# Expert results written to rows of their own, read back and summed at the end, in a GNN + mixture-of-experts kernel

## The chip, the cores and the metric

The kernel runs on one core of a Trainium2 chip. The metric is the device time of one execution in microseconds (us), smaller is better. Data are float32 throughout, except for a few index and bf16 helper tiles.

## The reference

Two layers over 1024 nodes of width 512. The first is a graph layer; the second is a mixture of 64 experts, of which each token takes the best two, with a small shared expert beside them:

```
x = x + relu(segment_sum(w[e] * (layernorm(x) @ W)[dst[e]], src[e]) + bias)   # 16384 edges
t = layernorm(x)                                                              # the ffn's input
scores = sigmoid(t @ Wg.T + bg);  w, idx = top_k(scores, 2);  w = w / w.sum(-1)
nx = layernorm(t)
y[token] = sum over its 2 experts e of  w_e * ( (silu(h1_e) * h3_e) @ W2_e + b2_e )
           h1_e = (nx*gamma_e + beta_e) @ W1_e + b1_e     # 512 -> 256
           h3_e = (nx*gamma_e + beta_e) @ W3_e + b3_e
z = shared expert of width 32;  out = x + y + z
```

So there are 1024 x 2 = 2048 pairs of token and expert, 32 for an expert on average. Each expert has 1.5 MB of weights (W1, W3 and W2 of 512 KB each), 96 MB in all, and each is read once.

## The kernel before, in words

The work has three stages. Up to about 130 us the graph layer is built from one-hot products. Up to about 190 us the tokens are routed: every token's two experts and weights are found, and a record (token, weight) is scattered to the DRAM table `slots`, in which each expert has a list of CAP = 80 entries (empty ones hold 60000). From about 193 us to the end the 64 experts run, in 8 groups (`GROUPS`) of 8 (`RING`). This last stage is the one that the change touches.

For each expert u of a group, five engines work in a chain, tied by semaphores:

- SP (SyncE) loads the expert's weights into a ring of 8 buffers (`load_expert`, lines 278 to 280). The load for the expert 8 further on is issued when the second matmul of this one is done (`y_ps`).
- POOL (GpSimd) gathers the 80 rows of the expert's tokens from `nx_rows` in DRAM by an indirect DMA (`gather`, line 443) into one of 8 buffers `xg`, six experts ahead (`AHEAD`). Empty entries lie past the bound and move nothing.
- PE (TensorE) transposes these rows (line 1074), multiplies by W1 and W3 (`up`, line 1098) and by W2 (`down`, line 1105). Its order is: rows of u+1, up of u, down of u-1.
- DVE (VectorE) applies gamma and beta (line 871) and forms silu(h1)*h3 (line 887). ACT (ScalarE) computes the silu (line 598) and, in `result` (line 607), scales the expert's result by the routing weight into one of 4 buffers `ysb`. Before it may overwrite one, it waits on `y_out` for the scatter of four experts earlier.
- POOL scatters `ysb` to the DRAM table `totals` with an accumulating indirect DMA (`scatter`, line 452). `totals` holds one row for each token, prefilled with the rest of the output (`store_x`, line 303), and 80 spare rows to which the empty entries go. Since two experts may add to the same row, each scatter first waits until the one before it has landed.

POOL runs all of its part in one order. For a step u of a group: gather(u+6), then scatter(u-1). At the start of each group it waits for its gathers and copies the gather indices (line 472), waits until all scatters of the group before have landed, copies the scatter indices (line 480), and only then issues gather(6) of the new group. After the last scatter SP copies `totals` from DRAM to the output in one DMA (line 324).

Of the kernel before, what the change touches and what calls it, by code (L numbers as in the profile page):

```python
# [6 lines left out]
N, D = 1024, 512  # L7
# [3 lines left out]
P = 128  # L11
NB = N // P
# [10 lines left out]
CAP = 80  # L23
# [3 lines left out]
RING = 8  # L27
GROUPS = EXPERTS // RING
XG, AHEAD = 8, 6
YS = 4  # L30
# [3 lines left out]
def moe_gnn(nc, x, src, dst, ew, W, bias, Wg, bg, gamma, beta, W1, b1, W3, b3, W2, b2,  # L34
# [11 lines left out]
    f32, i32, u32, bf16 = mybir.dt.float32, mybir.dt.int32, mybir.dt.uint32, mybir.dt.bfloat16  # L46
    ALU = mybir.AluOpType
# [5 lines left out]
    with ctx:  # L53
# [3 lines left out]
        def sem(name):  # L57
            return ctx.enter_context(nc.semaphore(name))
# [1 line left out]

        nx_rows = nc.dram_tensor("nx_rows", (N, D), f32).ap()
        slots = nc.dram_tensor("slots", (EXPERTS * LIST, REC), f32).ap()
        totals = nc.dram_tensor("totals", (N + CAP, D), f32).ap()


        w13 = sb("w13", [P, RING, 2, DC, HID])
        w2 = sb("w2", [P, RING, HC, D])
        X = sb("X", [P, NB, D])
        A = sb("A", [P, (N + WIN) * 8])
        HW = sb("HW", [P, NB, D])  # L70
# [16 lines left out]
        spare = sb("spare", [P, 1])  # L87
# [49 lines left out]
        before = GW[:, 0, 256:384]  # L137
        stackT = [GW[0:97, 2 + i // 4, 128 * (i % 4):128 * (i % 4) + 128] for i in range(NB)]
        late = A[:, :]
# [15 lines left out]
        idx_g = late[0:CAP, o + 192:o + 192 + RING + AHEAD].bitcast(i32)  # L155
        idx_s = late[0:CAP, o + 208:o + 208 + RING].bitcast(i32)

        mv1 = small[:, 0:16].rearrange("p (s a) -> p s a", a=2)
        ve = small[:, 16:32].rearrange("p (s a) -> p s a", a=2)
        rs = small[:, 32:48].rearrange("p (s a) -> p s a", a=2)  # L160
# [71 lines left out]
        xe_ps, xe_ready, h_ps, sl_ready, hT_ready, y_ps, y_ready = (sem(s) for s in (  # L232
            "xe_ps", "xe_ready", "h_ps", "sl_ready", "hT_ready", "y_ps", "y_ready"))
        y_out = [sem(f"y_out{i}") for i in range(YS)]
        x_out = sem("x_out")
        out_done = sem("out_done")
        held = sem("held")

        def hold(engine):

            engine.sem_inc(held, 1)
# [8 lines left out]
        def _(sp):  # L250
# [21 lines left out]
            sp.wait_ge(consts, 6)  # L272
            sp.dma_start(slots.rearrange("(p n) r -> p (n r)", p=P), sentinel).then_inc(sentinel_out, 16)

            sp.dma_start(totals[N:N + CAP, :], HW[0:CAP, 0, :]).then_inc(sentinel_out, 16)

            def load_expert(e, u):
                sp.dma_start(w13[:, u, 0, :, :].rearrange("p c h -> p (c h)"), W1v[e]).then_inc(w_in[u], 16)
# [18 lines left out]
                sp.wait_ge(rec_out[i], 32 * NB // 2)  # L297
            lists = slots.rearrange("(e n) r -> e (n r)", e=EXPERTS)

            def store_x(blocks):  # L300
                for s in blocks:
                    sp.wait_ge(z_added, s + 1)
                    sp.dma_start(totals[s * P:(s + 1) * P, :], X[:, s, :]).then_inc(x_out, 16)

            with sp.Fori(0, R2) as r:
                sp.dma_start(L, lists[:, ds(r * (CAP * REC), CAP * REC)]).then_inc(list_in, 16)
                with sp.If(r < 1):
                    store_x(range(NB))
                with sp.Fori(0, GROUPS - 1) as g:
                    for u in range(RING):  # L310
                        used = sp.snap(r * EXPERTS + g * RING + (u + 1))
                        e = sp.snap(g * RING + (RING + u))
                        sp.wait_ge(y_ps, used)
                        load_expert(e, u)
                with sp.If(r + 1 < R2):
                    for u in range(RING):
                        used = sp.snap(r * EXPERTS + (EXPERTS - RING + u + 1))
                        sp.wait_ge(y_ps, used)
                        load_expert(u, u)

            last = sp.snap(R2 * (16 * EXPERTS // YS))
            for i in range(YS):
                sp.wait_ge(y_out[i], last)
            sp.dma_start(out.rearrange("(p b) d -> p (b d)", p=P),
                         totals[0:N, :].rearrange("(p b) d -> p (b d)", p=P)).then_inc(out_done, 16)
            sp.wait_ge(out_done, 16)


        @block.gpsimd
        def _(pool):  # L330
# [12 lines left out]

            g.memset(rec, 0.0).then_inc(consts, 1)
            pool.wait_ge(consts, 7)
            g.iota(rec[:, :, :, 0], pattern=[[P, NB], [0, 2]], base=0, channel_multiplier=1,
                   allow_small_or_imprecise_dtypes=True).then_inc(consts, 1)
            pool_n = [0]

# [56 lines left out]
            def scatter_records(s):  # L406

                pool.wait_ge(rec_ready, s + 1)
                if s == 0:
                    pool.wait_ge(sentinel_out, 32)  # L410
                for k in range(2):
                    g.indirect_dma_start(slots, bass.IndirectOffsetOnAxis(ap=slot[:, s, k:k + 1], axis=0),  # L412
                                         rec[:, s, k, :], None).then_inc(rec_out[s % 2], 16)
# [29 lines left out]
                g.indirect_dma_start(xg[b], None, nx_rows, bass.IndirectOffsetOnAxis(ap=idx_g[:, col:col + 1], axis=0),  # L443
                                     bounds_check=N - 1, oob_is_err=False).then_inc(xg_in[b], 16)

            def scatter(u, count, before):

                pool.wait_ge(y_ready, count)
                if u:
                    pool.wait_ge(y_out[(u - 1) % YS], (before + (u - 1) // YS + 1) * 16)  # L450
                hold(pool)
                g.indirect_dma_start(totals, bass.IndirectOffsetOnAxis(ap=idx_s[:, u:u + 1], axis=0), ysb[u % YS], None,  # L452
                                     compute_op=ALU.add).then_inc(y_out[u % YS], 16)

            with pool.Fori(0, R2) as r:
                pool.wait_ge(list_ready, r + 1)
# [7 lines left out]
                def group(gi, first, last):  # L464
                    n = RING if last else RING + AHEAD
                    base = r * EXPERTS + gi * RING
                    before = r * (EXPERTS // YS) + gi * (RING // YS)

                    for b in range(AHEAD):
                        pool.wait_ge(xg_in[b], (r * GROUPS + gi + 1) * 16)  # L470
                    hold(pool)
                    g.tensor_copy(idx_g[:, 0:n], TOK[:, ds(gi * RING, n)]).then_inc(idx_copied, 1)
                    if first:
                        pool.wait_ge(x_out, 16 * NB)
                        hold(pool)
                    else:
                        for b in range(YS):
                            pool.wait_ge(y_out[b], before * 16)
                        hold(pool)
                    g.tensor_copy(idx_s[:, :], DROW[:, ds(gi * RING, RING)]).then_inc(idx_copied, 1)  # L480
                    pool.wait_ge(idx_copied, r * (2 * GROUPS + 1) + gi * 2 + 3)
                    hold(pool)
                    for u in range(RING):
                        if not (last and u >= RING - AHEAD):
                            if not first or u + AHEAD >= XG:

                                pool.wait_ge(xe_ps, base + (u + AHEAD - XG + 1))
                                hold(pool)
                            gather(u + AHEAD, (u + AHEAD) % XG)
                        if u:  # L490
                            scatter(u - 1, base + u, before)
                    scatter(RING - 1, base + RING, before)

                group(0, True, False)
                with pool.Fori(1, GROUPS - 1) as gi:
# [7 lines left out]
        def _(act):  # L503
# [17 lines left out]

            def x_times_w(g, u):
                act.wait_ge(hw_ps, g + 1)
                act.wait_ge(sentinel_out, 32)
                a.copy(HW[:, ds(g, 1), :].rearrange("p a n -> p (a n)"), bank[6 + u][:, :]).then_inc(hw_ready, 1)

            def pair(j, last):
# [95 lines left out]
        def _(dve):  # L623
# [231 lines left out]
            R2 = dve.value_load(rounds_sb[0:1, 1:2], min_val=1, max_val=ROUNDS)  # L855
            with dve.Fori(0, R2) as r:
                dve.wait_ge(list_ps, r + 1)
                v.tensor_copy(TOK, bank[6][0:CAP, 0:64])
                v.tensor_scalar(DROW, bank[6][0:CAP, 0:64], spare[0:CAP, :], None, ALU.min)
                v.tensor_copy(CW, bank[6][0:CAP, 64:128]).then_inc(list_ready, 1)  # L860
                with dve.If(r < 1):
                    for b in range(3, 6):
# [31 lines left out]
                group(GROUPS - 1, True)  # L894
                for i in range(YS):
                    dve.wait_ge(y_out[i], (r + 1) * (16 * EXPERTS // YS))

        @block.tensor
        def _(pe):
# [244 lines left out]
```

## Time and profile before

| | us |
|---|---|
| median of 3 runs | 652.58 |
| lowest and highest run | 644.8, 663.48 |
| span of the profiled execution, first to last instruction | 654.0 |

The profiled execution has no time listed apart from its span. Its span lies 1.4 us above the median of the runs. Of the span PE is busy 567.6 us (87%), POOL 233.9 us (36%), DVE 225.0 us (34%) and ACT 174.2 us (27%). PE's matmuls are pipelined, so that its busy time is no measure of its peak; the stretches in which it has no work at all, and those in which its clock is below 1.0, are what is to be looked for.

### The profile page before, as it was taken

To read this page: it belongs to the slowest core of one execution; us is meant where nothing else is said; L and a number is where in the kernel's file an instruction comes from. 1 tells how busy PE (TensorE), PEld (TensorE's weight loads), DVE (VectorE), ACT (ScalarE), POOL (GpSimd) and SP (SyncE) were. 2 spreads that over 40 slices of the span, in tenths; PEclk is the share of its full clock that TensorE was granted. 3 is DMA by queue.
4 is the path that set the end of the run, shared out by engine and by line. 5 is a ranking of instruction groups with operands and counts; after the bars stand their busy time and mean duration, and the time that the engine had idled before them with its cause. 6 is when DMAs were issued, how large, how long until landed. Compare 5 with 4: busy or idle time off the path is not lost. (4 is left out here: it accounts for less than half of the span.)

```text
span 654.0 us, 10918 instructions
## 1 busy us (share of the span) xinstructions
PE 567.6 (87%) x3327; PEld 425.4 (65%) x3328; DVE 225.0 (34%) x816; ACT 174.2 (27%) x399; POOL 233.9 (36%) x308
## 2 busy tenths in 40 slices
PE   4999999999639999899959999886997997799940
PEld 3666665566327888678846877665886785688820
DVE  5767622676744233222312322221232222122200
ACT  9698842232201212212202112110211121022110
POOL 3744401333625322332244232415323431542331
PEclk9899999999858999969968999895998899599975
DMA  5992001000013899969867998794998799494224
GB/s 171 407 401 85 0 5 42 33 18 32 33 40 125 270 319 305 287 201 325 283 185 230 308 299 272 235 299 133 289 317 264 214 295 307 84 324 127 40 30 148
DMA packets 53402, 127.23 MB, mean 195 GB/s; under 512 B 9832, under 2 KB 10408, under 8 KB 53218
## 3 DMA queue, kind: packets, MB, share of 16 engines
q1 hardware_dynamic: 42626, 112.24, 48.6%
q0 software_dynamic: 10752, 14.72, 13.3%
q8 instruction: 10, 0.16, 0.1%
q14 instruction: 14, 0.11, 0.1%
HBM read 117.82 MB, written 17.49 MB: 207 GB/s over the span
## 5 line engine op out<-in xcount | busy, mean ns | idle before, releaser
L1098 PE MATMUL bank<-A,w 128*128 128x80 f32 x2048 | 255.4, 286 | 0.0
L1098 PEld LDWEIGHTS bank<-A,w 128*128 128x128 f32 x2048 | 253.1, 204 | 0.5 <-issue 0.5
L452 POOL DMA_INDIRECT totals<-A x64 | 91.9, 1435 | 231.8 <-issue 141.5
L1105 PE MATMUL bank<-w,A 128*80 128x512 f32 x256 | 126.9, 626 | 3.3 <-DVE A L887 3.3
L871 DVE TENSOR_SCALAR A<-bank,gT,bT 128x80 f32<-128x80 f32 x256 | 74.6, 353 | 106.8 <-PE bank L1074 106.8
L887 DVE SCALAR_TENSOR_TENSOR A<-bank,b13T,A 128x80 f32<-128x80 f32 x128 | 32.6, 296 | 210.3 <-ACT A L598 210.3
L598 ACT ACTIVATE A<-bank,b13T 128x80 f32<-128x80 f32 x128 | 34.7, 323 | 237.3 <-PE bank L1098 237.3
L1074 PEld LDWEIGHTS bank<-ident,A 80*128 80x128 f32 x256 | 39.8, 210 | 63.3 <-DMA A<-nx_rows,A 36.3
L607 ACT ACTIVATE A<-bank,A 80x512 f32<-80x512 f32 x64 | 43.7, 682 | 116.1 <-PE bank L1105 67.4
L443 POOL DMA_INDIRECT A<-nx_rows,A x64 | 62.6, 978 | 26.2 <-issue 24.4
L1105 PEld LDWEIGHTS bank<-w,A 128*80 128x80 f32 x256 | 36.2, 160 | 47.2 <-issue 39.3
L1074 PE MATMUL bank<-ident,A 80*128 80x80 f32 x256 | 39.4, 278 | 30.1 <-DMA A<-nx_rows,A 30.1
L987 PE MATMUL bank<-HW,AT 128*128 128x512 f32 x128 | 57.3, 593 | 0.0
L513 ACT ACTIVATE osl<-iota,eT 128x128 f32<-128x128 f32 x128 | 39.0, 388 | 10.9 <-PE bank L950 10.9
L987 PEld LDWEIGHTS bank<-HW,AT 128*128 128x128 f32 x128 | 23.3, 190 | 23.9 <-issue 23.9
L957 PE MATMUL bank<-GW,xhT 128*128 128x512 f32 x64 | 29.7, 609 | 0.0
L715 DVE TENSOR_TENSOR A<-A,bank 128x384 f32 x32 | 17.7, 553 | 27.1 <-PE bank L950 23.9
L384 POOL TENSOR_SCALAR M<-iota,small 128x128 f32<-128x128 f32 x16 | 13.6, 852 | 24.8 <-PE bank L950 24.1
L950 PE MATMUL bank<-M,osl 128*128 128x128 f32 x128 | 20.2, 305 | 0.0
L412 POOL DMA_INDIRECT slots<-small,GW x16 | 16.5, 1029 | 10.3 <-DVE GW L833 6.3
L957 PEld LDWEIGHTS bank<-GW,xhT 128*128 128x128 f32 x64 | 12.0, 199 | 12.0 <-issue 12.0
L950 PE MATMUL bank<-AT,osl 128*128 128x128 f32 x128 | 19.3, 296 | 0.0
(166 smaller groups left out, 381.4 us busy)
## 6 DMA issues: line engine op xcount, KB each, us to landing
w<-in_L_ffn_W_dram SPq DMA_DIRECT2D x192, 512.0 KB, 5.9
X<-in_x_dram SPq DMA_DIRECT2D x4, 512.0 KB, 6.3
totals<-X SPq DMA_DIRECT2D x8, 256.0 KB, 2.9
GW<-in_L_gnn_W_dram SPq DMA_DIRECT2D x1, 1024.0 KB, 9.4
nx_rows<-osl SPq DMA_DIRECT2D x4, 256.0 KB, 2.0
nx_rows<-xh SPq DMA_DIRECT2D x4, 256.0 KB, 2.0
A<-nx_rows,A POOLq DMA_INDIRECT x64, 5.0
totals<-A POOLq DMA_INDIRECT x64, 5.1
```

The costliest lines, as they stand in the source:

```text
L443: g.indirect_dma_start(xg[b], None, nx_rows, bass.IndirectOffsetOnAxis(ap=idx_g[:, col:col + 1], axis=0), bounds_check=N - 1, oob_is_err=F ...
L452: g.indirect_dma_start(totals, bass.IndirectOffsetOnAxis(ap=idx_s[:, u:u + 1], axis=0), ysb[u % YS], None, compute_op=ALU.add).then_inc(y_ ...
L513: ins = a.activation(osl[:, h % 2, k, :], iota[:, :], ACT.Abs, bias=eT[:, 1, ds(j * 32 + 8 * h + k, 1)])
L598: ins = a.activation(sl[u % 2][:, m, :], bank[2 + u % 2][:, m * CAP:(m + 1) * CAP], ACT.Silu, bias=b13T[:, 0, m, ds(g * RING + u, 1)])
L607: a.activation(ysb[u % YS], bank[6 + u % 2][0:CAP, :], ACT.Copy, scale=CW[:, ds(g * RING + u, 1)]).then_inc(y_ready, 1)
L871: ins = v.tensor_scalar(xe[b][:, c, :], bank[b][:, c * CAP:(c + 1) * CAP], gT[:, c, ds(e, 1)], bT[:, c, ds(e, 1)], ALU.mult, ALU.add)
L950: ins = t.matmul(bank[q % 4][:, ds(at[k], TW)], osl[:, (q // 2) % 2, (q % 2) * QUAD + k, :], Mq[q % 4][:, k, :], start=False, stop=(k == Q ...
L957: ins = t.matmul(bank[6 + u][:, :], xhT[:, u, c, :], GW[:, c, :], start=(c == 0), stop=(c == DC - 1))
L987: ins = t.matmul(bank[4 + s % 2][:, :], AT[:, s % 2, k, :], HW[:, k, :], start=(k == 0), stop=(k == NB - 1))
L1074: ins = t.transpose(bank[u % 2][:, c * CAP:(c + 1) * CAP], xg[u % XG][:, c:c + DC * (P - 1) + 1:DC], ident[0:CAP, 0:CAP])
L1098: ins = t.matmul(bank[b][:, m * CAP:(m + 1) * CAP], w13[:, u, a, c, m * P:(m + 1) * P], xe[u % 2][:, c, :], start=(c == 0), stop=(c == DC ...
L1105: ins = t.matmul(bank[6 + u % 2][0:CAP, :], hT[u % 2][:, m, :], w2[:, u, m, :], start=(m == 0), stop=(m == HC - 1))
```

## The change

Each result now goes to a row of its own. The record of a token's first choice holds the token number, that of its second choice the token number plus 1024, and `totals` has 2048 rows. The scatter writes without accumulation and without a wait for the scatter before it, and empty entries lie past a bound, so they move nothing. DVE works out the token number from the record with one more instruction. `totals` is no longer prefilled: X with the shared expert's part stays in SBUF. At the end SP reads `totals` back in 8 DMAs of 512 KB (both rows of 128 tokens each) into weight buffers, DVE adds the two rows to X (two instructions for each block), and SP stores each block with a DMA of 256 KB. The waits at the start of a group, and ACT's wait on `y_out`, stay.

```
-        totals = nc.dram_tensor("totals", (N + CAP, D), f32).ap()
+        totals = nc.dram_tensor("totals", (2 * N, D), f32).ap()
...
+        token_of = late[0:CAP, o + 216:o + 280]
+        back = [w13[:, 2 + i // 2, i % 2, :, :].rearrange("p c h -> p (c h)").rearrange("p (k d) -> p k d", k=2) for i in range(NB)]
...
-            sp.dma_start(totals[N:N + CAP, :], HW[0:CAP, 0, :]).then_inc(sentinel_out, 16)
...
-                with sp.If(r < 1):
-                    store_x(range(NB))
...
-            sp.dma_start(out.rearrange("(p b) d -> p (b d)", p=P),
-                         totals[0:N, :].rearrange("(p b) d -> p (b d)", p=P)).then_inc(out_done, 16)
-            sp.wait_ge(out_done, 16)
+            for s in range(NB):
+                sp.dma_start(back[s], totals.rearrange("(k n) d -> n k d", k=2)[s * P:(s + 1) * P, :, :]).then_inc(back_in[s], 16)
+            for s in range(NB):
+                sp.wait_ge(x_final, s + 1)
+                sp.dma_start(out[s * P:(s + 1) * P, :], X[:, s, :]).then_inc(out_done, 16)
+            sp.wait_ge(out_done, 16 * NB)
...
-            g.iota(rec[:, :, :, 0], pattern=[[P, NB], [0, 2]], base=0, channel_multiplier=1,
+            g.iota(rec[:, :, :, 0], pattern=[[P, NB], [N, 2]], base=0, channel_multiplier=1,
...
-            def scatter(u, count, before):
+            def scatter(u, count):
                 pool.wait_ge(y_ready, count)
-                if u:
-                    pool.wait_ge(y_out[(u - 1) % YS], (before + (u - 1) // YS + 1) * 16)
                 hold(pool)
                 g.indirect_dma_start(totals, bass.IndirectOffsetOnAxis(ap=idx_s[:, u:u + 1], axis=0), ysb[u % YS], None,
-                                     compute_op=ALU.add).then_inc(y_out[u % YS], 16)
+                                     bounds_check=2 * N - 1, oob_is_err=False).then_inc(y_out[u % YS], 16)
...
-                    if first:
-                        pool.wait_ge(x_out, 16 * NB)
-                        hold(pool)
-                    else:
+                    if not first:
                         for b in range(YS):
                             pool.wait_ge(y_out[b], before * 16)
                         hold(pool)
...
-                v.tensor_copy(TOK, bank[6][0:CAP, 0:64])
-                v.tensor_scalar(DROW, bank[6][0:CAP, 0:64], spare[0:CAP, :], None, ALU.min)
+                v.tensor_scalar(token_of, bank[6][0:CAP, 0:64], float(N), -float(N), ALU.is_ge, ALU.mult).then_inc(second_half, 1)
+                v.tensor_copy(DROW, bank[6][0:CAP, 0:64])
+                dve.wait_ge(second_half, r + 1)
+                v.tensor_tensor(TOK, token_of, bank[6][0:CAP, 0:64], ALU.add)
...
+            for s in range(NB):
+                dve.wait_ge(back_in[s], 16)
+                link(v.tensor_tensor(X[:, s, :], back[s][:, 0, :], X[:, s, :], ALU.add))
+                v.tensor_tensor(X[:, s, :], back[s][:, 1, :], X[:, s, :], ALU.add).then_inc(x_final, 1)
```

## Rows read from the trace of the kernel before

**Rows 1.** The page's 40 slices: PE's busy tenths, granted clock in tenths

```profile
PE   4999999999639999899959999886997997799940
...
PEclk9899999999858999969968999895998899599975
```

**Rows 2.** Waits, whole span: engine, line, releaser: us in total, times, longest

```profile
POOL totals L452 <- DMA totals<-A: 62.2, 17, 5.6
ACT A L607 <- DMA totals<-A: 48.7, 15, 8.4
...
PEld bank L1074 <- DMA A<-nx_rows,A: 36.3, 8, 8.8
```

**Rows 3.** Timeline of PE, expert stage: start us, us, engine, line, count, idle before

```profile
203.35 3.76 PE L1098 MATMUL bank<-A,w 128*128 128x80 f32 x32
...
241.72 3.74 PE L1098 MATMUL bank<-A,w 128*128 128x80 f32 x32
...
249.16 3.74 PE L1098 MATMUL bank<-A,w 128*128 128x80 f32 x32
...
327.21 1.88 PE L1105 MATMUL bank<-w,A 128*80 128x512 f32 x4
336.37 0.81 PE L1074 MATMUL bank<-ident,A 80*128 80x80 f32 x4 [7.28 <-DMA A<-nx_rows,A]
336.97 7.03 PE L1098 MATMUL bank<-A,w 128*128 128x80 f32 x32
...
347.64 3.74 PE L1098 MATMUL bank<-A,w 128*128 128x80 f32 x32
...
621.21 3.69 PE L1098 MATMUL bank<-A,w 128*128 128x80 f32 x32
```

**Rows 4.** Timelines of ACT (first row) and POOL, experts 8 to 16

```profile
302.84 0.68 ACT L607 ACTIVATE A<-bank,A 80x512 f32<-80x512 f32 x1 [1.55 <-DMA totals<-A]
...
276.56 1.45 POOL L452 DMA_INDIRECT totals<-A  x1 [0.30 <-issue]
...
326.32 1.42 POOL L452 DMA_INDIRECT totals<-A  x1 [6.11 <-issue]
...
331.65 0.18 POOL L480 COPY A<-A 80x8 int32 x1 [3.71 <-DMA totals<-A]
332.93 1.01 POOL L443 DMA_INDIRECT A<-nx_rows,A  x1 [1.09 <-issue]
```

**Rows 5.** View of the tensor totals, 250 to 600 us

```profile
DMA to landing us min/median/max: 3.8/5.6/8.3
```

**Rows 6.** DMA views: whole span; 14 to 50 us; one stretch (engines, clock, DMA share, GB/s)

```profile
q1 hardware_dynamic: 42626, 112.24, 48.6%
q0 software_dynamic: 10752, 14.72, 13.3%
...
DMA packets 5071, 14.55 MB, mean 404 GB/s; under 512 B 436, under 2 KB 436, under 8 KB 4938
...
360.00:370.00 10.00, 10.00 (x78) 8.82 (x77) 3.26 (x12) 1.77 (x5) 2.41 (x2) 1.00 0.99 315
```

**Rows 7.** Timelines of ACT, POOL and SP, last two groups

```profile
593.04 0.68 ACT L607 ACTIVATE A<-bank,A 80x512 f32<-80x512 f32 x1 [1.31 <-PE bank L1105]
...
594.52 1.44 POOL L452 DMA_INDIRECT totals<-A  x1 [6.23 <-ACT A L607]
...
628.48 0.68 ACT L607 ACTIVATE A<-bank,A 80x512 f32<-80x512 f32 x1 [1.03 <-PE bank L1105]
...
641.22 1.40 POOL L452 DMA_INDIRECT totals<-A  x1 [3.28 <-DMA totals<-A]
645.22 0.63 SPq L324 DMA_DIRECT2D out_dram<-totals  x1
```

**Rows 8.** DVE: groups by line; timeline at 195.7 us

```profile
L837 DVE TENSOR_TENSOR X<-X,bank 128x512 f32<-128x512 f32 x8 | 5.2, 683 | 3.3 <-PE bank L1031 3.3
...
195.72 0.27 DVE L859 TENSOR_SCALAR A<-bank,spare 80x64 int32<-80x64 f32 x1
```

More of the change, by code:

```diff
@@ L234, in moe_gnn @@
         y_out = [sem(f"y_out{i}") for i in range(YS)]
-        x_out = sem("x_out")
+        back_in = [sem(f"back_in{i}") for i in range(NB)]
+        x_final = sem("x_final")
         out_done = sem("out_done")
+        second_half = sem("second_half")
         held = sem("held")
@@ L298, in _ @@
             lists = slots.rearrange("(e n) r -> e (n r)", e=EXPERTS)
[L300 to L303, printed above, removed]
             with sp.Fori(0, R2) as r:
                 sp.dma_start(L, lists[:, ds(r * (CAP * REC), CAP * REC)]).then_inc(list_in, 16)
-                with sp.If(r < 1):
-                    store_x(range(NB))
                 with sp.Fori(0, GROUPS - 1) as g:
@@ L409, in scatter_records @@
                 if s == 0:
-                    pool.wait_ge(sentinel_out, 32)
+                    pool.wait_ge(sentinel_out, 16)
                 for k in range(2):
@@ L490, in group @@
                         if u:
-                            scatter(u - 1, base + u, before)
-                    scatter(RING - 1, base + RING, before)
+                            scatter(u - 1, base + u)
+                    scatter(RING - 1, base + RING)
                 group(0, True, False)
@@ L523, in x_times_w @@
                 act.wait_ge(hw_ps, g + 1)
-                act.wait_ge(sentinel_out, 32)
+                act.wait_ge(sentinel_out, 16)
                 a.copy(HW[:, ds(g, 1), :].rearrange("p a n -> p (a n)"), bank[6 + u][:, :]).then_inc(hw_ready, 1)
```

## The prediction, made before the changed kernel ran

> **What bounds the kernel now.** I read the 40 slices of the page first [rows 1]. PE is at 9 tenths for most of the span, so the kernel looks bound by TensorE. But in the second half there are dips, and the clock row falls to 5 or 6 tenths near each. The list of waits says who makes them [rows 2]: PE's weight loads wait 36.3 us in 8 places for the DMA that gathers token rows. The same list shows POOL waiting 62.2 us for its own last scatter, and ACT waiting 48.7 us for a scatter to free its result buffer.
>
> The timeline of PE turns this into a floor [rows 3]. From the first product of expert 0 (203.35) to that of expert 8 (249.16) nothing stops it: 45.81 us for a group of 8, or 5.73 us an expert, at full clock. From expert 0 to expert 7 it is 38.37 us. Without a stop the last expert would start 7 x 45.81 + 38.37 = 359.0 us after the first, at 562.4. It starts at 621.21. So 58.8 us are lost.
>
> One stop shows how. PE starts the second product of expert 19 at 327.21, behind the first of expert 20; then it is idle 7.28 us until the rows of expert 22 are there (336.37). When it goes on, its clock is at the lower of its two levels (1.2 GHz instead of 2.4): the products of expert 21 take 7.03 us instead of 3.74, and from there to the next expert it is 347.64 - 336.97 = 10.67 us instead of 5.73, so 4.9 us more. I found the same pattern, a late row gather in the sixth step of a group, six times, with the lower clock after five of them; and one more stop, of 5.0 us in all, where ACT waited for a buffer. With the longer products behind each, the six cost 7.5, 12.6, 1.5, 12.2, 8.4 and 12.2 us (rows 3 show the second). All seven give 59.4 us, which agrees with the 58.8.
>
> Why is the gather late? POOL's timeline answers [rows 4]. The eight scatters of experts 8 to 15 start between 276.56 and 326.32, 7.1 us apart, while PE needs 5.73 for an expert. A scatter waits for the landing of the one before; with its issue of 1.45 us and a landing of 5.6 us in the median [rows 5] that is the 7.1. ACT had expert 15's result at 302.84 + 0.68 = 303.5, and its scatter starts at 326.32, 22.8 us late. Only after it has landed does POOL copy the new group's indices (331.65) and issue the gather of expert 22 (332.93), for which PE is already waiting. The chain of accumulating scatters sets the pace, by way of POOL's fixed order.
>
> **The change, part by part.** *The wait between scatters goes.* POOL's work for an expert is then one gather and one scatter, 1.01 + 1.45 us and 0.3 us before each: 3.1 us, against 5.73 for PE. POOL stops being late within a group. What stays is the start of a group: the last scatter, its landing, two copies, two gathers. In rows 4 the gather follows the last scatter after 332.93 - 326.32 = 6.6 us and the next scatter some 9 us after it; this is under two experts' time, and ACT has four buffers. How early is the gather of a group's seventh expert then? Expert 7's result is out when expert 8 starts, near 250, its scatter starts about 1 us later, the gather of expert 14 near 258, and it has landed by 263. PE wants those rows ahead of expert 13's product, five experts after 249.16, at about 276. There are 13 us of slack. ACT's wait for a buffer asks for a scatter four experts back, 4 x 5.73 = 22.9 us, against issue plus landing of about 7 to 10 us. So neither wait should ever end last, and the whole 58.8 us go, the low-clock stretches included, since in this trace (experts 0 to 12) the clock stays at 1.0 while PE has no stop. Bounds: nothing at all to 58.8; I take 58.8 because both slacks are larger than any landing shown (8.3 at most, rows 5).
>
> *What is late next?* PE itself, if DMA can follow. The weight queue moved 112.24 MB in 48.6% of 654 us [rows 6], 353 GB/s; 1.57 MB of weights are 4.5 us an expert. The indirect queue took 13.3%, 87 us, or 1.3 us for each of 64 experts. Together 5.8 us, which fills PE's 5.73, and the stretch at 360 us indeed shows a DMA share of 0.99. Afterwards the indirect queue moves fewer bytes: gathers 2048 rows of 2 KB (4.2 MB), scatters 2048 rows instead of 64 x 80 = 5120 (4.2 MB instead of 10.5): 8.4 instead of 14.7 MB. By bytes alone that is 0.8 us an expert, 5.3 in all; an add costs more than a write if anything. So DMA drops below PE's pace, with 8% to spare, and landings should get shorter. If scatters were no cheaper than now, DMA would lose 0.07 us an expert, 5 us in all: that is a bound for the range.
>
> *The prefill goes* (8 stores of 256 KB before the first expert, and 160 KB at the start). Nobody on the path waits for them: the list of waits has no line in which POOL or PE waits for the prefill. I cost it at nothing, 0 to 1 us of gain. The weight loads behind them on SP's queue wait for PE anyway.
>
> *DVE's extra instruction* stands before the first gathers. Its like takes 0.27 us [rows 8]; with the semaphore I take +0.3 us. PE is covered by the shared expert's matmuls until the first rows come, so it is 0 to 0.6.
>
> *The end.* Now: ACT's last result is out at 628.48 + 0.68 = 629.16 [rows 7], but the scatters lag behind by 12 us, and the last starts at 641.22; SP issues the output copy at 645.22, and the end is at 654.0. That is 24.8 us after the result. Afterwards: a scatter starts 0.8 us after its result when POOL is free (593.04 + 0.68 to 594.52), and 4.0 us after its start SP goes on (641.22 to 645.22): 4.8 us. Then 4.2 MB are read and 2.1 MB written. The largest stretch of plain loads of this size ran at 404 GB/s [rows 6]: 6.3 MB are 15.6 us. The output copy's 8.8 us for 2.1 MB (5.2 us at that rate) leave 3.5 us of fixed cost, so 19 us. DVE gives nearly the same: first block landed after 3.5 + 1.3, then 8 blocks x 2 adds x 0.68 us [rows 8] plus 0.1 for the link, 11.7 us, then one store's 2 to 3 us: 19. The end takes 4.8 + 19 = 23.8 us, 1.0 less than now. The drain of the chain pays for the reading back. Bounds: 3 us better, if an unaccumulated scatter lands sooner; 5 us worse at 315 GB/s [rows 6].
>
> The Trainium skill (DMA: Bandwidth & Descriptors, Rules for kernel authors) speaks against this end: it wants at least 1 MiB in a DMA for full bandwidth, and the change cuts 6 MB into pieces of 512 and 256 KB. By its figure for 1 MiB, 341 GB/s, the end would cost about 3 us more, as an estimate. The 512 KB weight loads of the trace, queued back to back, already reach 404 GB/s, so I stay with the row.
>
> **Sum.** 654.0 - 58.8 - 1.0 + 0.3 = 594.5 for the profiled execution. The median of the runs lies 1.4 under its span, so I say 594. The runs before spread from 644.8 to 663.5; since the floor holds no stop, I expect less spread now.
>
> **The rivals.** *Part of the stops stay* (615). The start of a group still waits for its last scatter to land, and if landings stay long or POOL is slower than I think, two of the six groups still have a stop of about 10 us (58.8 / 6): 594.5 + 20. For it speaks that the wait is left in the code; against it the 13 us of slack. *The landing is the cause, not the chain* (about 652, no change): rows come late since DMA is full, whoever issues them. For it: the share of 0.99 at 360 us. Against it: the late gather was issued at 332.93 and PE started at 336.37, 3.4 us later, so it was issued late and not landed late. This is also the case in which the change doesn't do what it says. *Slower* (about 670): the reading back runs at half the rate, some 200 GB/s, since it reads rows that were just scattered in pieces of 2 KB: 6.3 MB take 31 us instead of 16, 15 to 16 us more. Alone it would only bring the forecast to 610; it decides the sign only if at the same time under 15 us of the stops go. For it speaks only that no row shows such a read; against it that a third of the weight loads in the stretch at 404 GB/s, those of W2, are rows of 2 KB as well.
>
> **How the numbers follow.** Forecast 0.82 (587 to 604), part of the stops 0.11, no change 0.03, slower 0.02, and 0.02 for better than 587. The range reaches from 587 (landings and end at their good bounds, run spread) to 610 (end 5 worse, DMA 5 worse, half a stop). About 2% is what a measurement here can tell from no change, 13 us. Faster by more: 0.95; within: 0.03; slower: 0.02.
>
> **What would show it.** In the profile after: POOL no longer waits for the last scatter before the next one; scatters 5.7 us apart; no wait of PE for row gathers, and ACT none for a result buffer; clock at 1.0 from the first expert to the last; the last expert's product starts about 359 us after the first; q0 moves about 8.4 MB; DMA share in the stage near 0.9; from the last result to the end about 24 us. The prediction is wrong if PE waits for weights, if its clock falls without a stop, or if the end takes over 30 us.

## The result and the profile after

The changed kernel takes 596.29 us (median of 4 runs, 595.27 to 596.83) against 657.92 us for the kernel before (4 runs): a ratio of 0.919, 95% interval 0.909 to 0.929. The profiled execution has a span of 593.2 us and a time of 595.27 us. The forecast was 594, with a span of 594.5.

The page's slices and queues of the changed kernel:

```profile
PE   2999999999973799999999999999999999999940
...
PEclk9999999999995799999999999999999999999975
DMA  5995001010110158888889888878978878880029
...
q1 hardware_dynamic: 44658, 114.17, 54.5%
q0 software_dynamic: 8704, 8.44, 4.4%
...
PE 89%; DVE 4%; DMA 3%; issue 2%; POOL 1%; SPq 0%; ACT 0%; POOLq 0%; ACTq 0%
```

In [rows 1] PE had dips and a falling clock from the second third on. Now both rows are full from the first expert to the last. The last row is the chain of work that ended last: 89% of the span is now PE. The timeline of PE, expert stage:

```profile
203.86 3.80 PE L1098 MATMUL bank<-A,w 128*128 128x80 f32 x32
...
249.75 3.74 PE L1098 MATMUL bank<-A,w 128*128 128x80 f32 x32
...
276.24 0.59 PE L1074 MATMUL bank<-ident,A 80*128 80x80 f32 x4
...
562.44 3.69 PE L1098 MATMUL bank<-A,w 128*128 128x80 f32 x32
```

From the first expert to the last it is 358.6 us; before it was 417.9 [rows 3]. No product takes more than 3.8 us. The rows of expert 14 are transposed at 276.24 without any idle time in front, at the place where the kernel before had its late gathers. The waits, whole span (engine, line, releaser: us in total, times, longest):

```profile
POOL totals L449 <- ACT A L601: 159.3, 45, 4.9
ACT A L601 <- PE bank L1105: 71.6, 61, 1.3
...
POOL A L474 <- DMA totals<-A: 41.1, 7, 6.9
```

POOL's scatter now waits for ACT's result, and ACT for PE; the waits of [rows 2] for a landing, for a free buffer and for gathered rows are gone. One wait for a landing is left, that at a group's start (line 474, seven times, 5.9 us each). POOL's timeline shows it:

```profile
249.34 0.96 POOL L449 DMA_INDIRECT totals<-A  x1 [3.49 <-ACT A L601]
251.10 0.94 POOL L449 DMA_INDIRECT totals<-A  x1 [0.80 <-issue]
252.04 0.20 POOL L469 COPY A<-A 80x14 int32 x1
259.04 0.18 POOL L474 COPY A<-A 80x8 int32 x1 [6.80 <-DMA totals<-A]
260.30 1.00 POOL L442 DMA_INDIRECT A<-nx_rows,A  x1 [1.07 <-PE bank L1074]
```

The last scatter of group 0 starts at 251.10, and the gather of expert 14 only 9.2 us later. PE wants those rows at 276.24, so it doesn't matter. The end:

```profile
569.72 0.68 ACT L601 ACTIVATE A<-bank,A 80x512 f32<-80x512 f32 x1 [1.03 <-PE bank L1105]
571.27 0.91 POOL L449 DMA_INDIRECT totals<-A  x1 [0.66 <-issue]
573.83 4.02 SPq L321 DMA_DIRECT2D w<-totals  x8
577.30 0.69 DVE L895 TENSOR_TENSOR X<-w,X 128x512 f32<-128x512 f32 x1 [9.94 <-DMA w<-totals]
...
588.44 0.69 DVE L896 TENSOR_TENSOR X<-w,X 128x512 f32<-128x512 f32 x1
```

From the last result (569.72 + 0.68 = 570.40) to the end it is 22.8 us; before it was 24.8 [rows 7].

### The profile page after: what moved, and what is told of

The parts are those of the page before. It is cut to its first block, busy times and chain, and to the rows that moved or that the text cites. A ratio compares the mean times of both kernels' runs of the same rounds, so it can differ in the third digit from the quotient of the medians.

```text
span 593.2 us, 10987 instructions
## 1 busy us (share of the span) xinstructions
PE 541.4 (91%) x3327; PEld 407.7 (69%) x3328; DVE 235.6 (40%) x833; ACT 174.2 (29%) x399; POOL 202.2 (34%) x308
## 3 DMA queue, kind: packets, MB, share of 16 engines
q0 software_dynamic: 8704, 8.44, 4.4%
## 4 chain that ended last, share of the span: by engine, by line
PE 89%; DVE 4%; DMA 3%; issue 2%; POOL 1%; SPq 0%; ACT 0%; POOLq 0%; ACTq 0%
PE bank L1098 39%; PE bank L1105 18%; PE bank L987 9%; PE bank L950 6%; PE bank L1074 5%; PE bank L957 5%; PE bank L947 2%; PE bank L975 1%; PE bank L1031 1%; DMA w<-totals 1%; DMA X<-in_x_dram 1%; PE bank L1006 1%; PE bank L933 1%; DVE X L896 1%; DVE X L895 1%
## 5 line engine op out<-in xcount | busy, mean ns | idle before, releaser
L1098 PE MATMUL bank<-A,w 128*128 128x80 f32 x2048 | 239.2, 275 | 0.0
L1098 PEld LDWEIGHTS bank<-A,w 128*128 128x128 f32 x2048 | 237.1, 194 | 0.6 <-issue 0.5
L449 POOL DMA_INDIRECT totals<-A x64 | 60.7, 948 | 179.4 <-ACT A L601 159.3
L1105 PE MATMUL bank<-w,A 128*80 128x512 f32 x256 | 119.2, 593 | 0.0
L1105 PEld LDWEIGHTS bank<-w,A 128*80 128x80 f32 x256 | 34.0, 151 | 40.3 <-issue 35.7
L507 ACT ACTIVATE osl<-iota,eT 128x128 f32<-128x128 f32 x128 | 39.1, 388 | 13.3 <-PE bank L950 12.3
L1074 PE MATMUL bank<-ident,A 80*128 80x80 f32 x256 | 38.1, 271 | 0.0
```

The costliest lines, as they stand in the source:

```text
L507: ins = a.activation(osl[:, h % 2, k, :], iota[:, :], ACT.Abs, bias=eT[:, 1, ds(j * 32 + 8 * h + k, 1)])
L1074: ins = t.transpose(bank[u % 2][:, c * CAP:(c + 1) * CAP], xg[u % XG][:, c:c + DC * (P - 1) + 1:DC], ident[0:CAP, 0:CAP])
L1098: ins = t.matmul(bank[b][:, m * CAP:(m + 1) * CAP], w13[:, u, a, c, m * P:(m + 1) * P], xe[u % 2][:, c, :], start=(c == 0), stop=(c == DC ...
L1105: ins = t.matmul(bank[6 + u % 2][0:CAP, :], hT[u % 2][:, m, :], w2[:, u, m, :], start=(m == 0), stop=(m == HC - 1))
```

## The experiments

Each set was timed beside the kernel before on one chip. "Step" is the time from one scatter's start to the next. "Round" is the time from the first scatter of a group to that of the next, the mean of seven; at PE's full pace it is 45.8 us. Round and stage are read from one profiled execution of each kernel. "Stage" is the time from PE's product for expert 0 to that for expert 63. "Landing" is the median, over the scatters between 250 and 520 us, of the time from the start of the DMA instruction to its landing; the time that POOL needs to issue it is part of it.

```
run              time us  ratio to before (95%)      round  stage  landing
before           652-658  1                          56.1   417.9  6.2
changed          596.3    0.919 (0.909 to 0.929)     45.8   358.6  6.5
e1_chain         603.1    0.919 (0.911 to 0.928)     48.2   365.1  4.7
e2_order         640.9    0.975 (0.964 to 0.986)     53.6   402.8  5.9
e3_skip          643.5    0.982 (0.972 to 0.991)     54.4   407.2  6.1
e4_acc           598.8    0.915 (0.908 to 0.922)     46.0   358.5  6.9
f1_after_w       597.1    0.915 (0.907 to 0.923)     45.8   358.6  5.4
f2_before_w      753.6    1.156 (1.146 to 1.166)     69.5   514.5  7.5
f3_skip_w        729.4    1.118 (1.109 to 1.128)     66.3   491.3  6.8
e7_rows80        596.7    0.914 (0.907 to 0.922)     46.1   358.6  6.4
g1_before_late   626.3    0.952 (0.948 to 0.957)     51.7   385.6  4.8
g2_skip_late     617.3    0.939 (0.933 to 0.944)     50.3   381.2  4.7
g3_after_late    596.7    0.907 (0.902 to 0.912)     45.8   358.6  3.8
e5_ahead3        665.3    1.012 (1.006 to 1.018)     54.9   429.0  5.7
```

The kernel before ran at medians of 654.9, 655.6 and 657.6 us beside the three sets, so ratios of different sets differ by half a per cent for that alone. The gains of e2_order (2.5%) and e3_skip (1.8%) are clear of zero, but their intervals include 2%; e5_ahead3 lies within 2% of the kernel before.

### The changed kernel with the wait back (e1_chain)

```
-            def scatter(u, count):
+            def scatter(u, count, before):
...
+                if u:
+                    pool.wait_ge(y_out[(u - 1) % YS], (before + (u - 1) // YS + 1) * 16)
...
```

> The changed kernel with one thing undone: each scatter again waits until the one before has landed. Rows of their own, no add, the skipped empties and the new end all stay. Theory (the wait between scatters set the pace): in the changed kernel a plain scatter takes 0.96 us to issue and 6.5 us in the median to land, so a chain of them runs at 7.5 us for an expert against PE's 5.73; the late gathers, the waits for a result buffer and the low clock come back, and the time is 640 to 660. Rival (fewer bytes and no add did it): landings are short enough for the chain to keep PE's pace, and the time stays at 597 to 602.

603 us: next to the rival's 597 to 602, and a miss for my theory. With the wait back, the stage is only 6.5 us longer; PE's loads wait 4.4 us in all for gathers. The view of the tensor `totals` between 250 and 520 us shows why:

```profile
DMA to landing us min/median/max: 2.3/4.7/7.6
```

At its shortest a plain scatter lands 2.3 us after its start, against the 6.5 us on which the theory had built. In the last group, where no weights are loaded any more, chained scatters start 3.2 us apart wherever the wait for the landing ends last:

```profile
553.26 0.95 POOL L451 DMA_INDIRECT totals<-A  x1 [0.30 <-issue]
556.54 0.94 POOL L451 DMA_INDIRECT totals<-A  x1 [2.33 <-DMA totals<-A]
```

In the last group of the kernel before they start 4.7 us apart, and with the empties skipped but the adds kept (e3_skip) 4.3 to 4.6. So on a quiet DMA the accumulating scatter costs about 1.5 us more a step than a plain one (0.48 of it POOL's issue, 1.44 us against 0.96). The round goes from 56.1 to 48.2 us, most of the way to 45.8. This run skips the empties too; skipping alone takes the round to 54.4 (e3_skip), so that most of the gain, though not all, belongs to the plain write. A chain of plain scatters that write all 80 rows was not run.

### The kernel before with two gathers moved forward (e2_order)

```
                     g.tensor_copy(idx_g[:, 0:n], TOK[:, ds(gi * RING, n)]).then_inc(idx_copied, 1)
+                    pool.wait_ge(idx_copied, r * (2 * GROUPS + 1) + gi * 2 + 2)
+                    hold(pool)
+                    for u in range(2):
+                        if not first:
+                            pool.wait_ge(xe_ps, base + (u + AHEAD - XG + 1))
+                            hold(pool)
+                        gather(u + AHEAD, (u + AHEAD) % XG)
...
-                        if not (last and u >= RING - AHEAD):
+                        if u >= 2 and not (last and u >= RING - AHEAD):
```

> The kernel before with one thing moved: at the start of a group POOL issues the gathers of the group's seventh and eighth expert before it waits for the old group's scatters. The chain of accumulating scatters stays. Theory (the chain's pace is the bound, and the late gather only the place where it shows): PE no longer waits for row gathers, but ACT waits for result buffers and PE for ACT; at some 7 us a scatter the stage takes no less than its 421 us of before, and the time is 645 to 680. Rival (POOL's fixed order at the group's start is the cause): the stops go and the time is 600 to 615.

641 us, 4 under the theory's range and 26 over the rival's. The round is 53.6 us; ACT's wait for result buffers rises from 48.7 us to 68.6 us, PE's loads still wait 26.8 us for gathers (five times). The gather of a group's seventh expert now follows the last scatter after 2.7 us (321.23 and 323.95) instead of 6.6, but that scatter is as late as before. POOL's order at this point was worth 15 us of stage (417.9 to 402.8); the other 44 us above 358.6 stay with the chain.

### The kernel before with empties skipped (e3_skip)

```
-                v.tensor_scalar(DROW, bank[6][0:CAP, 0:64], spare[0:CAP, :], None, ALU.min)
+                v.tensor_copy(DROW, bank[6][0:CAP, 0:64])
...
-                                     compute_op=ALU.add).then_inc(y_out[u % YS], 16)
+                                     bounds_check=N - 1, oob_is_err=False, compute_op=ALU.add).then_inc(y_out[u % YS], 16)
```

> The kernel before with one thing changed: the empty entries of a scatter lie past a bound and move nothing, so it adds 32 rows on average in place of 80. Accumulation, chain and end stay. Theory: the landing is mostly latency behind the weight loads and not the scatter's own bytes, so the chain runs at over 6.3 us and the time is 630 to 655. Rival (the bytes of the empty rows made the chain slow): landings fall by more than 1.5 us, the chain keeps 5.73 us, and the time is 595 to 615.

643 us, as the theory had it, 1.8% less than before. The scatters' bytes fall by 60% and the indirect queue's share from 13.3% to 7.2%, yet the landing is 6.1 us against 6.2. The bytes of the empty rows are a small part of a landing. Skipping them gains a little in every chained pair of runs, though: 655 to 643, 754 to 729 (f2, f3) and 626 to 617 us (g1, g2).

### Accumulation without the wait (e4_acc)

```
+            def prefill():
+                sp.wait_ge(zero_ready, 1)
+                for s in range(NB):
+                    sp.dma_start(totals[N + s * P:N + (s + 1) * P, :], HW[:, 0, :]).then_inc(x_out, 16)
+                for s in range(NB):
+                    sp.wait_ge(z_added, s + 1)
+                    sp.dma_start(totals[s * P:(s + 1) * P, :], X[:, s, :]).then_inc(x_out, 16)
...
-                                     bounds_check=2 * N - 1, oob_is_err=False).then_inc(y_out[u % YS], 16)
+                                     bounds_check=2 * N - 1, oob_is_err=False, compute_op=ALU.add).then_inc(y_out[u % YS], 16)
...
-                link(v.tensor_tensor(X[:, s, :], back[s][:, 0, :], X[:, s, :], ALU.add))
-                v.tensor_tensor(X[:, s, :], back[s][:, 1, :], X[:, s, :], ALU.add).then_inc(x_final, 1)
+                v.tensor_tensor(X[:, s, :], back[s][:, 0, :], back[s][:, 1, :], ALU.add).then_inc(x_final, 1)
```

> The changed kernel with accumulation back but no wait between scatters: the first row of a token is prefilled with X and the shared expert's part, the second with zeros (16 stores of 256 KB before the first scatter), scatters add onto rows that no other scatter touches, and the end has one add for a block in place of two. Theory (accumulation costs nothing by itself, the wait it needed did): the expert stage takes 359 us as in the changed kernel; the end, which there is set by 16 DVE adds of 0.72 us, becomes bound by the reads (10.4 us for 4.2 MB at 404 GB/s) and falls from 22.8 to about 20 us; time 592 to 595. Rival (adding scatters load DMA so that rows or weights come late): PE waits in the stage again, over 600.

The stage is as expected (358.5 us, no stop), with the longest landing of all unstopped runs. So accumulation costs the stage nothing once nobody waits for it in turn. The time, 598.8 us, lies above the theory's 592 to 595. The end is the miss: the last scatter lands later (4.8 us from the last result to the reads, against 3.4), and from the issue of the reads to the end of the span it takes 20.2 us (575.59 to 595.8) with half the adds, against 19.4 in the changed kernel (573.83 to 593.2). DVE now sits idle between blocks:

```profile
579.10 0.69 DVE L912 TENSOR_TENSOR X<-w 128x512 f32<-128x512 f32 x1 [11.35 <-DMA w<-totals]
...
583.94 0.69 DVE L912 TENSOR_TENSOR X<-w 128x512 f32<-128x512 f32 x1 [0.66 <-DMA w<-totals]
585.29 0.69 DVE L912 TENSOR_TENSOR X<-w 128x512 f32<-128x512 f32 x1 [0.66 <-DMA w<-totals]
```

Three of the seven gaps between blocks are 1.35 us, which is 512 KB at 388 GB/s; the mean is 1.55 us, with the stores of finished blocks in between. From 579 to 591 us DMA is busy at its full share. In the changed kernel it is too (577 to 589 us), though DVE has no pause there either from 581.02 on. Since half the adds did not shorten the end, reads and stores together, 6.3 MB, bind it, and not the adds.

### Weight loads tied to the scatter (f1_after_w, f2_before_w, f3_skip_w)

The same edit in the changed kernel, in the kernel before, and in e3_skip:

```
                         sp.wait_ge(y_ps, used)
+                        sp.wait_ge(scattered, used)
                         load_expert(e, u)
...
+                pool.sem_inc(scattered, 1)
```

The increment stands right behind the scatter's `indirect_dma_start`.

> The changed kernel with one wait added for SP: it issues the three weight loads into a freed buffer only when POOL has issued the scatter of the same expert. In the changed kernel the loads go out first and the scatter 0.2 us behind the third, and every scatter of the stage takes 5.7 to 7.6 us to land. Theory (a landing is long since 1.57 MB of weights, 3.9 us at 404 GB/s, were queued just ahead of it): the median landing falls from 6.5 to 2.5 to 4 us, POOL's wait at a group's start from 5.9 us to under 4; the time stays within 1% of 596, since PE has no stop either way. Rival (the landing is long since the core's DMA is 85% busy at all times, or since a write to DRAM is slow): the median stays over 5.5 us.

> The kernel before, chain, accumulation, empties and old end all kept, with the same wait for SP: weights of the freed buffer are loaded only behind the issue of that expert's scatter. Theory (a chain of scatters stops PE only while its step, issue and landing, is longer than PE's 5.73 us; the loads ahead of a scatter make it so): without loads ahead of it the step is about 4.7 to 5.5 us, the stops go, the stage takes 359 to 370 us, and since the old end is short (last result to end: about 17 us) the time is 585 to 605. Rival (the wait between scatters is bad whatever the loads do, or accumulation of 80 rows is too slow): the step stays over 6.3 us and the time over 630.

> As the run before it, and the empty entries skipped by a bound as in the earlier run: chain and accumulation of 32 rows on average, weights behind the scatter, old end. Theory: the step is as short or shorter, the time 583 to 600. Rival (as before): over 630.

The edit did not do what it was meant to do, and that made it the sharpest run of the study. Here are POOL and SP of f2_before_w:

```profile
304.11 1.44 POOL L454 DMA_INDIRECT totals<-A  x1 [5.50 <-issue]
304.13 0.33 SPq L279 DMA_DIRECT2D w<-in_L_ffn_W_dram  x1
304.56 0.38 SPq L280 DMA_DIRECT2D w<-in_L_ffn_W_dram  x1
305.03 0.38 SPq L281 DMA_DIRECT2D w<-in_L_ffn_W_dram  x1
...
312.53 1.43 POOL L454 DMA_INDIRECT totals<-A  x1 [5.69 <-issue]
312.55 0.33 SPq L279 DMA_DIRECT2D w<-in_L_ffn_W_dram  x1
```

SP's loads go out 0.02 us after the scatter has started, while POOL still needs 1.4 us to issue it. At the first scatter of a group, right behind two gathers, they go out even 1.3 us ahead of it (356.63 and 357.92). The increment that stands behind the scatter in the program did not wait for it. So 1.57 MB of weights, 3.9 us at 404 GB/s [rows 6], now go out beside every scatter before POOL is through with it, and the step is 8.3 us in the mean of the first seven groups, 3.6 more than the 4.7 of a quiet stretch. The round rises to 69.5 us, the stage by 97 us, the time by 16%. No engine waits for weights in this run: PE's stops are waits for gathers (96 us) and for DVE's product (11 us), and ACT waits 225 us for result buffers.

The kernel before shows the same cost by itself. Of its 49 steps in the first seven groups, 12 have no weight load issued from 4 us before the scatter's start to 1.6 us after it; these take 4.6 to 4.8 us. The other 37 take 5.1 to 9.1 us, 7.3 in the mean. Here are five scatters in a row; the next loads after 330.6 us go out at 347.55, 347.98 and 348.45:

```profile
335.54 1.45 POOL L452 DMA_INDIRECT totals<-A  x1 [0.30 <-issue]
340.23 1.44 POOL L452 DMA_INDIRECT totals<-A  x1 [1.97 <-DMA totals<-A]
344.89 1.43 POOL L452 DMA_INDIRECT totals<-A  x1 [1.94 <-issue]
349.61 1.44 POOL L452 DMA_INDIRECT totals<-A  x1 [2.00 <-issue]
357.22 1.44 POOL L452 DMA_INDIRECT totals<-A  x1 [4.90 <-issue]
```

In f2 the suspected cost falls on every step, and the time follows. With skipped empties (f3) the step is 7.9 and the time 729.

In the changed kernel (f1) the same edit moves the landing from 6.5 to 5.4 us, between what theory and rival expected, and the time not at all. No one waits there in turn.

### The changed kernel with all 80 rows written (e7_rows80)

```
-                v.tensor_copy(DROW, bank[6][0:CAP, 0:64])
+                v.tensor_tensor(DROW, bank[6][0:CAP, 0:64], spare2[0:CAP, :], ALU.min)
...
```

`spare2` holds 80 spare rows for each expert, and the scatter's bound is raised to include them.

> The changed kernel, but a scatter writes all of its 80 rows, the empty ones to spare rows of their own for each expert (10.5 MB in place of 4.2). Theory (DMA has room): the indirect queue rises from 4.4% to some 8 to 9% of the span, DMA's share in the stage from 0.86 to 0.92, PE has no stop, time 594 to 600. Rival (the change gained by the bytes it no longer moves): stops come back, over 610.

As the theory had it in time and stops; the indirect queue takes less than its 8 to 9%. One row for the stretch from 250 to 500 us of each kernel (busy of PE, PEld, DVE, ACT, POOL; clock, DMA share, GB/s); the changed kernel:

```profile
250.00:500.00 250.00, 250.00 (x1757) 203.70 (x1756) 72.96 (x264) 52.79 (x132) 86.30 (x100) 1.00 0.85 299
```

and the one with 80 rows:

```profile
250.00:500.00 250.00, 250.00 (x1757) 203.83 (x1756) 72.70 (x262) 53.19 (x131) 86.95 (x100) 1.00 0.91 315
```

DMA's share rises from 0.85 to 0.91 and PE sees nothing of it. The indirect queue takes 6.9% of the span for the same 14.72 MB that took 13.3% before [rows 6], so that with the adds its DMA time was about double. The cleaner pair is e4_acc against the changed kernel, the same 8.4 MB with and without adds: 6.9% of 595.8 us against 4.4% of 593.2, 41 us against 26.

### Weight loads really behind the scatter (g1_before_late, g2_skip_late, g3_after_late)

As before, but the signal comes from a small POOL instruction, which runs only after the scatter has been issued; in g1 in the kernel before, in g2 in e3_skip, in g3 in the changed kernel:

```
-                pool.sem_inc(scattered, 1)
+                g.memset(tick, 0.0).then_inc(scattered, 1)
+                pool.wait_ge(scattered, count)
+                hold(pool)
```

> The kernel before with its chain and accumulation, and SP's weight loads held until a small POOL instruction behind the expert's scatter has run, so really behind its issue of 1.44 us. (In the two runs before, the signal went out as the scatter started, 0.02 us ahead of it, so the loads still went in front of every scatter, and its landing rose to 7.5 us.) Theory (the chain's step is 4.7 us plus what of the 3.9 us of weights lies in front of the scatter): the step comes down to PE's pace of 5.73 us or a bit over it, few stops stay, and the time is 590 to 620. Rival (loads in flight slow a scatter wherever they were issued): the step stays over 6.5 us and the time over 640.

> The same, and the empty entries skipped by a bound. Theory: like the run before it or better, 585 to 610; with no stop left it would beat the changed kernel, since its end is 5 us shorter (one copy of 2.1 MB in place of 6.3 MB). Rival: over 635.

> The changed kernel with the same hold of the weight loads. Theory: the median landing of a scatter falls from 6.5 us to under 4.5 us and POOL's wait at a group's start with it; the time stays within 1% of 596, since that wait is covered. Rival: the landing stays over 5.4 us.

In g1 the chain, the adds and the 80 rows are all as before, and only the place of the loads differs (and POOL has one tiny instruction more a step): 626 us, a ratio of 0.952, and 0.831 of f2's time. g2 has 617. Both are above the range of the theory, though below the rival's. The round is 51.7 and 50.3 us, not 45.8: a scatter that comes late now meets the loads of the one before it, issued 2 to 3 us ahead, and the steps of g1 alternate in most groups between 4.8 us and 6.6 to 8.6 us. Loads issued 1.7 us or more after a scatter's start mostly do not lengthen it: 19 of 23 such steps of g1 take 4.6 to 4.9 us. So the place of the loads is confirmed as a cause, but this cure is a partial one. In g3 the landing falls to 3.8 us, as expected, and the time stays.

```profile
284.73 0.96 POOL L452 DMA_INDIRECT totals<-A  x1 [2.85 <-ACT A L607]
285.66 0.09 POOL L454 MEMSET A<- 1x1 f32 x1
285.98 0.33 SPq L283 DMA_DIRECT2D w<-in_L_ffn_W_dram  x1
```

This is g3: the loads go out 1.25 us after the scatter's start. In the changed kernel the third load stands 0.6 us in front of the scatter (288.92 and 289.56).

### Gathers three experts ahead (e5_ahead3)

```
-XG, AHEAD = 8, 6
+XG, AHEAD = 8, 3
```

> The changed kernel with the rows gathered three experts ahead in place of six. At a group's start POOL still waits for the last scatter, so the first gather of a group is then that of its fourth expert, which PE wants three experts or 17 us earlier than the seventh's. Theory (the wait at the group's start is hidden by a slack of 10 to 13 us, and by nothing else): the slack is short by 4 to 7 us at each of seven starts, and each stop brings some 4.5 us of low clock: time 645 to 680. Rival (the wait at the group's start costs nothing now that the chain is gone): 595 to 600.

665 us, in the middle of the theory's range. This is the changed kernel, without a chain, and it is 1.2% slower than the kernel before (1.006 to 1.018). POOL and PE at the start of group 1:

```profile
259.32 1.00 POOL L442 DMA_INDIRECT A<-nx_rows,A  x1 [1.39 <-issue]
...
265.71 0.81 PE L1074 MATMUL bank<-ident,A 80*128 80x80 f32 x4 [7.17 <-DMA A<-nx_rows,A]
266.32 7.04 PE L1098 MATMUL bank<-A,w 128*128 128x80 f32 x32
```

The gather goes out after the last scatter's landing, as in the changed kernel, and PE starts on its rows 6.4 us later. It stops 7.2 us, and each of the seven such stops (2.6 to 8.0 us) is followed by a product at the lower clock (7.03 to 7.04 us, 1.2 GHz). The wait that the change left in place costs 70 us of stage when the gathers run three ahead and nothing when they run six ahead.

## Why the prediction was right

**The 58.8 us of stops.** The step said that all go. Measured: the stage went from 417.9 to 358.6 us, 59.3 us less, against a predicted 359.0. The floor was read from one undisturbed group; the changed kernel and the four variants that have no stop agree on 358.6 to 0.1 us, 0.4 under it.

**Why they go.** The prediction put it on the wait between scatters, and e4_acc (adds, no wait, no stop) bears this out: taking the wait away is enough. What it did not see is that the plain write would nearly have been enough too (e1_chain, 6.5 us of stage). By these runs a chain stops PE only when seven steps and the one across a group's start take more than 45.8 us. Before, that was 7 x 6.7 + 9.2 = 56.1 us in the mean. The step is a base (4.7 us with adds, 3.2 us without, on a quiet DMA) plus what the weights in front add, 3.6 us in the mean of f2; the longest steps before, 9.1 us, are not fully explained by this. The prediction's rival "the landing is the cause, not the chain" was wrong as a forecast, but half of it was true: f2 and g1 move only the place of the loads and change the time by +16% and -5%.

One sum of the prediction came out by luck. It made the 7.1 us a scatter out of an issue of 1.45 us and a landing of 5.6 us. But the view counts a landing from the start of the instruction, so that the issue was counted twice: the scatter at 607.14 us has a landing of 4.0 us, and the next starts at 611.92, 0.8 us after it. The step is landing plus 0.8 to 0.9 us. The 7.1 us belong to group 1, and the 5.6 us are the median of a longer stretch with quiet groups in it. The time of the forecast does not rest on this sum, but the expectation for e1_chain repeated it (0.96 + 6.5 us).

**The start of a group.** The prediction had the gather 6.6 us behind the last scatter, shorter landings, and 13 us of slack. Measured: 9.2 us, landings of 6.5 us in the median instead of 5.6, and 276.2 - 260.3 - 6.4 = 9.5 us of slack (the 6.4 is from e5_ahead3). The error came from thinking that landings follow the DMA load. Unchained scatters start right behind the loads that the same event released, all of them in the stretch measured; 12 of the 49 chained ones had none near them. The slack was still enough, so it cost nothing.

**DMA.** Predicted 8.4 MB and 0.8 us an expert in the indirect queue, share near 0.9; measured 8.44 MB, 4.4% of 593.2 us or 0.4 us an expert, share 0.85.

**The start.** +0.3 predicted. The first product starts 0.5 us later than before, a single difference of two executions.

**The end.** Predicted 4.8 + 19 = 23.8 us. Measured 570.40 to 573.83, 3.4 us, since a plain scatter lands sooner (SP goes on 2.6 us after its start, not 4.0), and 19.4 us for reading back, adding and storing. The price of DMA was right; e4_acc shows that DVE's equal figure was not the one that binds. With the stage (59.3 us less), the end (2.0 less) and the start (0.5 more) the profiled span of 593.2 us is accounted for. The 512 KB reads came as fast as 388 GB/s, so that the Trainium skill's 1 MiB (DMA: Bandwidth & Descriptors, Rules for kernel authors) is not needed when pieces are queued back to back.

**The spread.** Less was expected; it is 1.6 us, against 18.7 before. The median is 2.3 us above the forecast, since time lies 2.1 us above the span in the profiled run. The 1.4 us that the prediction took off compared the span of one execution with the median of others; wherever a run has both, its time lies 1.7 to 2.3 us above its span.

## What to carry to other kernels

Read a floor from one stretch without a stop, count it out to the end, and what is missing is what a change can win; then ask for each wait left in the code how much slack covers it, and by what constant. A serial chain of DMAs costs its step, and here a step was 4.7 us by itself and up to some 4 us more for what was queued in front: look at which event releases both the bulk loads and the small transfer. To learn which half of a change did the work, undo each half alone; here either half would have done for most of it (603 us with the wait kept, 599 us with the adds kept).

## What the runs showed of the hardware

- A scatter of 80 rows of 2 KB takes POOL 1.44 us to issue with accumulation and 0.96 us without, whether the empty rows are skipped or not. Chained on a quiet DMA, scatters start 4.6 to 4.8 us apart with adds (last group of the kernel before), 4.3 to 4.6 with adds and skipped empties (e3_skip), 3.1 to 3.3 as skipped plain writes (e1_chain).
- With adds, the same 14.72 MB of gathers and scatters took 13.3% of 654 us of the DMA engines' time, without 6.9% of 594.6 us (e7_rows80): 87 against 41 us. The figure with adds moves with the traffic beside it: 76 us in f2_before_w, 94 us in g1_before_late.
- Bulk loads of 1.57 MB issued in the first 1.3 us of a scatter lengthen the step by nearly their own transfer time: 8.3 us in f2_before_w against 4.7 us. Issued 1.7 us or more after its start, in g1_before_late, they leave it at 4.6 to 4.9 us in 19 of 23 steps.
- A semaphore increment placed behind an indirect DMA in POOL's program released SP 0.02 us after the start of that DMA, 1.4 us before POOL was through with it, and 1.3 us before its start when gathers stood right in front (f2_before_w). An increment carried by a small compute instruction behind the DMA released SP 1.25 us after the start of a DMA of 0.96 us (g3_after_late).
- In the kernel before, PE's products ran at the lower clock for some 10 us after each of five stops for want of rows (2.4 to 8.0 us idle), and for some 3 us after a stop of 3.3 us for DVE's product; a stop of 1.2 us was not followed by it. The length of the stop alone doesn't tell: in e2_order one of 1.6 us was followed by a product of 7.04 us, in g1_before_late one of 0.9 us by a product of 5.41 us.
